# Later output turns, a moved PSUM bank and a shifted order of chunks in an attention and FFN kernel

## The reference

```python
x = x + xattn(layernorm(x), ctx, mask, padding)     # 32 query heads, 8 key groups, head size 16
#   q = X @ Wq.T + bq; k, v = ctx @ Wk.T + bk, ctx @ Wv.T + bv
#   w = softmax(where(mask, -inf, q k / 4)); out = (w v) @ Wo.T + bo
x = x + ternary_ffn(layernorm(x))                   # 512 -> 2048 -> 512
#   linear(x, w, g): rmsnorm(x) * g, rounded to 8 bits per token, times round(tanh(w / mean|w|))
#   h = silu(linear(x, w1)) * linear(x, w2); linear(h, w3)
x = x + attention_over_the_sequence(layernorm(x), ctx, ctx)
x = x + gated_ffn(layernorm(x))
```

## Time and profile before

| | us |
|---|---|
| median of 3 runs | 1564.48 (1561.67 to 1566.96) |
| profiled execution | 1560.04 |
| its span, first to last instruction | 1558.2 |
| busy PE, DVE, ACT, POOL | 1388.9, 806.3, 728.5, 481.5 |
| mean granted TensorE clock | 0.962 of full |

### The profile page before, as it was taken

How to read it: one execution, slowest core, us unless ns; L and a number is a source line. 1 busy time by engine, 2 the same in 40 slices (tenths; PEclk the granted TensorE clock), 3 DMA queues, 4 the chain that set the end, 5 groups by cost and what they waited for, 6 DMA issues and landing times. The chain is left out here.

```text
span 1558.2 us, 22502 instructions
## 1 busy us (share of the span) xinstructions
PE 1388.9 (89%) x8434; PEld 662.8 (43%) x8434; DVE 806.3 (52%) x1312; ACT 728.5 (47%) x1364; POOL 481.5 (31%) x522
## 2 busy tenths in 40 slices
PE   4788888788868999996899999989999999999998
PEld 4455555554533444552222222234444444444443
DVE  5864666566655878765666666624513211321220
ACT  3266666667664777771555555553501211210210
POOL 7211111446675775771322232144600000000000
PEclk9699999999988999997899999999999999999999
DMA  6646655656332010122644443223502002001000
GB/s 179 136 138 174 142 146 172 152 111 155 113 122 81 28 41 28 42 84 66 170 137 123 123 125 114 97 82 111 173 0 82 1 1 81 0 0 54 0 1 27
DMA packets 89446, 140.68 MB, mean 90 GB/s; under 512 B 8408, under 2 KB 47896, under 8 KB 88800
## 3 DMA queue, kind: packets, MB, share of 16 engines
q1 hardware_dynamic: 76544, 114.16, 26.8%
q10 hardware_dynamic: 12800, 25.17, 5.2%
HBM read 105.85 MB, written 33.46 MB: 89 GB/s over the span
## 5 line engine op out<-in xcount | busy, mean ns | idle before, releaser
L1785 DVE TENSOR_REDUCE c_negmax<-c_psA 128x1 f32<-128x512 f32 x256 | 165.7, 682 | 91.5 <-PE c_psA L1860 87.1
L2071 ACT ACTIVATE d_silu<-d_psGU 128x512 f32<-128x512 f32 x64 | 38.2, 596 | 344.3 <-PE d_psGU L2138 344.3
L2138 PE MATMUL d_psGU<-d_zt_hi,d_w_hi 128*128 128x512 bf16 x512 | 194.6, 380 | 3.8 <-ACT d_silu L2071 2.3
L2138 PE MATMUL d_psGU<-d_zt_hi,d_w_lo 128*128 128x512 bf16 x512 | 194.8, 380 | 0.0
L2138 PE MATMUL d_psGU<-d_zt_lo,d_w_hi 128*128 128x512 bf16 x512 | 194.8, 380 | 0.0
L1740 ACT ACTIVATE c_probs<-c_psB 128x512 f32<-128x512 f32 x256 | 140.4, 595 | 101.5 <-PE c_psB L1873 101.4
L2101 DVE TENSOR_TENSOR d_h<-d_psGU,d_silu 128x512 f32<-128x512 f32 x64 | 44.2, 691 | 221.2 <-PE d_psGU L2138 220.9
L894 DVE TENSOR_REDUCE a_negmax<-a_psX 128x4 f32<-128x1024 f32 x128 | 150.7, 1215 | 7.8 <-PE a_psX L1161 7.8
L753 ACT ACTIVATE a_probs<-a_psB 128x512 f32<-128x512 f32 x256 | 138.2, 593 | 24.8 <-PE a_psB L1173 24.5
L1860 PE MATMUL c_psA<-c_ks,c_qs 96*128 96x512 bf16 x256 | 103.8, 408 | 16.5 <-DVE c_negmax L1785 8.1
L672 POOL TENSOR_SCALAR ternary<-a_tern_stage 128x512 bf16<-128x512 f32 x48 | 91.6, 1924 | 77.4 <-ACT a_tern_stage L741 77.1
(11 more groups left out here) (231 smaller groups left out, 2559.0 us busy)
## 6 DMA issues: line engine op xcount, KB each, us to landing
a_tern_stage<-in_w ACTq DMA_DIRECT2D x32, 768.0 KB, 5.5
d_weight_stage<-in_w_last SPq DMA_DIRECT2D x24, 512.0 KB, 4.2
a_ks<-k_scr SPq DMA_DIRECT2D x8, 768.0 KB
a_qs<-q_scr SPq DMA_DIRECT2D x8, 768.0 KB
c_ks<-k_scr SPq DMA_DIRECT2D x48, 128.0 KB, 2.6
c_qs<-q_scr SPq DMA_DIRECT2D x48, 128.0 KB, 3.0
a_xz<-in_x SPq DMA_DIRECT2D x32, 128.0 KB, 3.1
a_ctx<-in_ctx_t SPq DMA_DIRECT2D x8, 512.0 KB, 4.7
```

The source lines that it names most:

```text
L1785: v.tensor_reduce(negm[:, u:u + 1], A[:, u % 2, :], AX.X, ALU.max, negate=True)\
L2138: last = pe.matmul(GU[:, 2 * up + i % 2, :], wgu[wh][:, i, up, k, :], zt[zh][:, k, :], start=(k == 0 and j == 0), stop=(k == DC - 1 and j ...
```

## The change

- Masked attention, order: in odd groups PE's `turn` goes from in front of the second scores to the end, in front of `weigh`, and DVE's `normalise` behind all reductions of the group. ACT's `out_high` goes from the start of an odd group to behind `results` of the even group before it (for the last chunk: from group 1 to group 0).
- Masked attention, inputs: DVE's statistics go from group 6 to 5, POOL's `scales` from 7 to 6 (in front of the additions of the output bias), ACT's `normalise` from the end of group 7 to the end of group 6.
- PSUM: keys and values are projected into bank 3 of X, not 2, and wait for the last maximum of the batch before and not for the copy of the transposed maxima. `transpose_max(b, 1)` goes behind the `turn` of group 0. The total of the weights' absolute values moves to a free corner of bank 2.
- Prologue: POOL's `inputs(1)` goes in front of `scales(1)`; DVE's `queries_low(1, 0)` and `(1, 1)` go between the first reductions.
- Ternary FFN: the down product of a chunk comes two parts after its transposition, not one; the x transposes go from part 1 to part 2. ACT takes the first x chunk after the first `scaled`, DVE the second after `largest(t, 0)`, and DVE's `update(t - 3)` goes from in front of `largest(t - 1, 1)` to behind `gate(t, 1)`.

```diff
@@ -441,7 +441,7 @@
...
         by_query = TURNED.rearrange("p (t r d) -> p t r d", t=ST, r=SHARE)
-        TOT = X[:, 3, 0:3]
+        TOT = X[:, 2, 300:303]
         MT = X[0:2 * HU, 2, :].bitcast(BF16)[:, 0:QJ * P]
@@ -636,8 +636,8 @@
...
                 g.memset(v1[i][:], 1.0).then_inc(s["ident"], 1)
+            inputs(1)
             scales(1)
-            inputs(1)
             g.memset(keep["ones"][:], 1.0).then_inc(s["ident"], 1)
@@ -656,7 +656,7 @@
...
                         inputs(b + 3)
-                    if grp == 7 and b + 3 < BATCH:
+                    if grp == 6 and b + 3 < BATCH:
                         scales(b + 3)
@@ -714,7 +714,7 @@
...
                 need(act, s["k_out"], n * 3 * DMA)
-                act.activation(k_hi[:], X[:, 2, 0:SEQ], ACT.Identity, bias=keep["bk"][:]).then_inc(s["k_hi"], 1)
+                act.activation(k_hi[:], X[:, 3, 0:SEQ], ACT.Identity, bias=keep["bk"][:]).then_inc(s["k_hi"], 1)
@@ -760,10 +760,6 @@
...
                     to, e = (b, 2 * g + 2) if g + 1 < GROUPS else (b + 1, 0)
-                    if g == 1 and b:
-                        out_high(b - 1, DC - 1)
-                    if g in (3, 5, 7):
-                        out_high(b, (g - 3) // 2)
                     if to < BATCH:
@@ -784,6 +780,10 @@
...
                     results(b, g)
+                    if g == 0 and b:
+                        out_high(b - 1, DC - 1)
+                    if g in (2, 4, 6):
+                        out_high(b, g // 2 - 1)
                     if b == TOTAL_AT and g == 1:
@@ -792,7 +792,7 @@
...
                         front.rounded(act, g - GROUPS + 2)
-                    if g == 7 and b + 3 < BATCH:
+                    if g == 6 and b + 3 < BATCH:
                         normalise(b + 3)
@@ -874,14 +874,14 @@
...
                 dve.wait_ge(s["k_hi"], n + 1)
-                v.scalar_tensor_tensor(out=k_lo[:], in0=X[:, 2, 0:SEQ], scalar=keep["bk"][:], in1=k_hi[:],
+                v.scalar_tensor_tensor(out=k_lo[:], in0=X[:, 3, 0:SEQ], scalar=keep["bk"][:], in1=k_hi[:],
                                        op0=ALU.add, op1=ALU.subtract).then_inc(s["k_lo"], 1)
...
                 v.tensor_tensor(v1[n % 3][:, :, :, 0:HD],
-                                X[:, 2, SEQ:2 * SEQ].rearrange("p (t g d) -> p t g d", t=ST, d=HD),
+                                X[:, 3, SEQ:2 * SEQ].rearrange("p (t g d) -> p t g d", t=ST, d=HD),
                                 keep["bv"][:].rearrange("p t (g d) -> p t g d", d=HD), ALU.add).then_inc(s["v_ready"], 1)
@@ -925,9 +925,9 @@
...
                         reduce_unit(b + 1, u)
-                    if g >= 1:
+                    if g % 2 == 0 and g:
                         normalise(b, g - 1)
-                    elif b:
+                    elif g == 0 and b:
                         normalise(b - 1, GROUPS - 1)
@@ -938,9 +938,11 @@
...
                         reduce_unit(b + 1, u)
+                    if g % 2:
+                        normalise(b, g - 1)
                     if more and g == 4:
                         split_max(b + 1, 0)
-                    if g == 6 and b + 3 < BATCH:
+                    if g == 5 and b + 3 < BATCH:
                         inputs(b + 3)
@@ -1026,10 +1028,10 @@
...
             second_ones()
-            queries_low(1, 0)
-            queries_low(1, 1)
             for u in range(HU):
                 reduce_unit(0, u)
+                if u < 2:
+                    queries_low(1, u)
             split_max(0, 0)
@@ -1089,15 +1091,15 @@
...
                 if n >= 2:
-                    pe.wait_ge(s["mt_copied"], 2 * (n - 1))
+                    pe.wait_ge(s["max_done"], MU * (n - 1))
                 for k in range(DC):
                     for i, (h, lo) in enumerate(halves):
-                        pe.matmul(X[:, 2, 0:SEQ], w[h, "wk"][:, k, :], (c_lo if lo else c_hi)[:, k, :],
+                        pe.matmul(X[:, 3, 0:SEQ], w[h, "wk"][:, k, :], (c_lo if lo else c_hi)[:, k, :],
                                   start=(k == 0 and i == 0), stop=(k == DC - 1 and i == 2))
...
                         for i, (h, lo) in enumerate(halves):
-                            last = pe.matmul(X[:, 2, SEQ + t * P:SEQ + (t + 1) * P],
+                            last = pe.matmul(X[:, 3, SEQ + t * P:SEQ + (t + 1) * P],
                                              (c_lo if lo else c_hi)[:, k, t * P:(t + 1) * P], w[h, "wv"][:, k, :],
@@ -1121,13 +1123,15 @@
...
-                    pe.wait_ge(s["v_ready"], min(b + 4, BATCH))
                     if b + 1 < BATCH:
...
                         pe.wait_ge(s["x_updated"], ST * b)
-                elif b + 1 == TOTAL_AT:
-                    pe.wait_ge(s["total"], 3)
+                    if b + 1 == TOTAL_AT:
+                        pe.wait_ge(s["total"], 3)
+                else:
+                    pe.wait_ge(s["v_ready"], min(b + 4, BATCH))
                 for k in range(DC):
@@ -1205,7 +1209,6 @@
...
                             turn_rows(n)
-                        transpose_max(b, 1)
                     if g == 1 and n is not None:
@@ -1214,16 +1217,19 @@
...
                         transpose_max(b + 1, 0)
-                    if g >= 1:
+                    if g % 2 == 0 and g:
                         turn(b, g - 1)
-                    elif b:
+                    elif g == 0 and b:
                         turn(b - 1, GROUPS - 1)
+                    if g == 0:
+                        transpose_max(b, 1)
                     if to < BATCH:
...
                         pe.wait_ge(s["total"], 1)
+                        pe.wait_ge(s["mt_copied"], 2 * (b + 1))
                         pe.matmul(TOT, keep["ones"][:], tot[:], start=True, stop=True).then_inc(s["total"], 1)
@@ -1231,6 +1237,9 @@
...
                         max_unit(b + 1, u)
+                    if g % 2:
+                        turn(b, g - 1)
                     weigh(b, g)
@@ -1434,9 +1443,9 @@
...
                     gate(t, 2)
-                take("x", t + 1, 0)
                 if 1 <= t <= NT:
                     scaled(t - 1, 0)
+                take("x", t + 1, 0)
                 if now:
@@ -1499,22 +1508,23 @@
...
                     gate(t, 0)
-                if t >= 3:
-                    update(t - 3)
                 if 1 <= t <= NT:
...
                     gate(t, 1)
+                if t >= 3:
+                    update(t - 3)
                 take("h", t - 2, 1)
...
                     gate(t, 2)
-                take("x", t + 1, 1)
                 next(ahead, None)
...
                     largest(t, 0)
+                take("x", t + 1, 1)
+                if now:
                     gate(t, 3)
@@ -1568,12 +1578,14 @@
...
                         product(t, n, 1, V, "h_done", "v_done")
-                    down(t - 3, NF - 1) if n == 0 else down(t - 2, n - 1)
-                    transposed("h", t - 2, n)
-                    if n == 1:
+                    down(t - 3, n + 2) if n < 2 else down(t - 2, n - 2)
+                    if n == 2:
                         for j in range(2):
                             transposed("x", t + 1, j)
-            down(NT - 1, NF - 1)
+                    transposed("h", t - 2, n)
+            for n in range(2, NF):
+                down(NT - 1, n)
 def build_sequence_attention(nc, io, keep, x_out, front, following):
```

## The result

The changed kernel takes 1556.13 us (median of 11 runs, 1551.73 to 1560.53), the kernel before 1565.38 in the same comparison (11 runs, 1561.15 to 1566.96). The ratio is 0.9944 (0.993 to 0.9958): about 9 us. The forecast had 18.5. Its sign was right and its range held the time, but the size was twice the true one.

A forecast was written before the change was run, and what follows sets the result against it. DVE's work was taken to pace attention groups 3 to 7 and a ring through POOL the FFN loop; savings of 2.0 + 8.4 + 1.8 + 0.5 + 5.9 = 18.6 us gave 1546 us, range 1531 to 1558.5.

The forecast's parts named there:

- Prologue: Before the attention: POOL's copies start at 29.65 in place of 31.76 us once its context split goes first; -2.0 us.
- Attention, group 3: Earlier `out_high`, then ACT binds: -0.1 us in each of batches 1, 2, 3, 5, 6; -1.0 in batch 0; -0.7 in batch 4.
- Groups 5 to 0: Attention: earlier inputs delay group 7, repaid by ready rows and keys in bank 3; -0.45 us for each of five batches.
- Batches 5 and 6: Attention without next inputs: transposed maxima behind the turn and group 1's late turn give 0.3 + 0.6 us each; -1.8.
- Late turning: Odd attention groups: late `turn` and `normalise` fall where PE waits for reductions anyway; 0, or 0.75 us a time without cover.
- FFN loop: Ternary FFN: PE's waits must go, but little becomes time; -0.3 us for each of six pairs of tiles, -1.8.
- ring through GpSimd: FFN loop: POOL's factors, ACT's rounding, DVE's gate and reductions, POOL again; closed by 28.8 us for two tiles.
- Tail: FFN drain of tiles 14 and 15: copy latency vanishes, the last tile's scale becomes the limit; -5.9 us.
- (a): Rival, FFN loop: PE's waits are the time; 9.8 us more gain, 1536 us; chance 0.13.
- (b): Rival, attention: all four waits are time; 41.7 us in place of 8.4, 1513 us; chance 0.05.
- (c): Rival, attention: it gives nothing, DVE and weight pieces bind; 1554 us, or 1557 with a smaller tail; chance 0.17.
- (d): Rival, odd attention groups: late `turn` idles DVE, 1.5 us in each of 21 groups; slower, 1586 us; chance 0.06.

The follow-up runs named there:

- e09: The kernel before with only GpSimd's `inputs(1)` put in front of `scales(1)`: 1560.88 us, 0.9975 of the kernel before.
- e13: The changed kernel with residual rows' loads cut to an eighth of their columns from batch 1 on: 1552.44 us, 0.9922 of the kernel before.
- e03: The changed kernel with ScalarE's one weight third in group 3 put behind the second exponentials and the results: 1547.15 us, 0.9876 of the kernel before.
- e04: The changed kernel with input statistics, scales and normalising back in groups 6, 7 and 7: 1548.51 us, 0.9897 of the kernel before.
- e10: The changed kernel with the edits of e03 and e04 together: 1537.95 us, 0.9833 of the kernel before.
- e08: The changed kernel loading an eighth of the columns of each FFN weight piece from the third on: 1547.03 us, 0.9896 of the kernel before.
- e05: The changed kernel with ScalarE's `out_high` back at the start of the odd groups: 1559.77 us, 0.9973 of the kernel before.
- e11: The changed kernel with the edits of e03, e04 and e06 together: 1536.75 us, 0.9824 of the kernel before.
- e06: The changed kernel with the odd groups' turning and normalising early again, in the even groups' place: 1549.26 us, 0.9909 of the kernel before.
- e14: The changed kernel with only VectorE's FFN `update` put back behind the first gate: 1579.98 us, 1.0092 of the kernel before.
- e12: The changed kernel with only ScalarE's normalising of batch b+3 back in group 7: 1551.76 us, 0.9915 of the kernel before.
- e02: The kernel before with only the edits of the ternary FFN, on all three engines: 1555.64 us, 0.9947 of the kernel before.
- e15: The changed kernel with only TensorE's order of the FFN products put back: 1603.77 us, 1.0250 of the kernel before.

## Why the prediction was half right

**Prologue (-2.0): right in size, by another course.** -2.6 in the profile, 3.9 with an interval of 2.0 to 5.8 in e09. GpSimd's copies start at 30.38 us, not at 29.65, as VectorE's mask copy came 0.7 later. VectorE's two copies of the constant rows and GpSimd's last one after are

```profile
33.05 6.49 DVE L998 COPY a_qs<-ones_row 32x8192 bf16<-32x8192 bf16 x1
39.46 9.10 DVE L999 COPY a_ks<-ones_row 32x8192 bf16<-32x8192 bf16 x1
```

```profile
37.33 9.08 POOL L646 COPY a_qs<-a_qs 64x8192 bf16<-64x8192 bf16 x1
```

where before VectorE's first began at 40.43 us and its second was

```profile
47.79 2.28 DVE L997 COPY a_ks<-ones_row 32x8192 bf16<-32x8192 bf16 x1
```

Before, only the first of VectorE's two collided with a copy of GpSimd, and now both do. GpSimd's last copy takes 2.1 us longer and ends 0.7 us later than before though it began earlier (46.41 for 45.72), while VectorE's last ends 1.5 us earlier (48.56 for 50.07), again 2.15 behind GpSimd's. The reductions follow on VectorE itself, so the gain is there, and not in GpSimd's copies, where the forecast had it. The Trainium skill (SBUF — State Buffer, the rule on the port pair) has the one that comes second stand still until the first is done; the 9.08 us of GpSimd's copy, which stood 7 us before, agree with it.

**Attention, group 3 (-0.5, -1.0, -0.7): the step that failed.** The forecast saw that "ACT then binds", and that its next third waits for a weight piece until 203.38, and gave 0.1 us a batch with the ends "nothing, and the full waits". Two things in it were wrong. It took the landing at 203.38 for fixed; it became 205.05, of which e13 puts 1.0 us to the residual loads that now go 2.8 us earlier. And it left out that all else on ScalarE stands in order behind that third and is needed earlier now. For batches 1 to 3, 5 and 6 together (groups 2 to 4) the term was -0.5; it is +3.8 in the pair of profiles, and between nothing and +4.6 when the three profiles of each attention are compared. With the third out of the way it is 7 to 9 us less than before (e03). Batch 0 gave 0.6 of its 1.0 in the pair, but took 48.2 to 52.5 us where the three profiles of before have 48.8 to 49.7; batch 4 lost 4.6 where 0.7 was to be won, in part by its groups 5 to 7 and by the clock. That the term could turn round could have been read from the profile: ScalarE's wait of 1.71 us in the earlier trace rows was hidden only as long as what it held up was needed later than it ended, and the edit made it needed 1.5 us earlier.

**Groups 5 to 0 (-0.45 for each batch): near as a sum, wrong in worth.** Counting from `weigh` of group 0, the forecast had `weigh` of group 6 at 37.9 us, of group 7 at 43.4 and of the next batch at 49.6. Less the 2.6 us lost in group 4, the changed kernel has 37.5, 43.8 and 49.9. In those terms a batch has 0.3 us more than forecast. But e04 shows that the edit was worth a loss: without it a batch takes 48.1 to 48.9 us (e10), with it 50.3 to 50.7 (e03). The forecast compared with the kernel before alone, and never with the change less this part; a part whose sum comes out near nothing is a part to look at by itself.

**Batches 5 and 6 (-1.8): half of it.** -0.8 in the pair, and -0.9 with groups 2 to 4 left out. The -4.1 of e03 and e08 lies almost all in groups 2 to 4, which this term was not about. **Batch 7 (-2.2): right**, 37.76 to 35.40 (35.4 to 36.1 for 37.3 to 37.8 in the six profiles). **Behind it**, from the last `weigh` to the last output product, 2.3 us went that no term had (11.3 to 9.0; 2.3 to 3.4 in the six profiles). Before, TensorE paused for 2.97 us and was at half clock from 464 to 470 us (granted 0.50), so that the first nine matmuls of the output product start some 0.43 us apart; e05, with the same pause, has the same. In the changed kernel that pause is 1.02 us, the clock is full (1.00 from 467 to 473) and they start 0.216 apart. The first two of before and of after:

```profile
467.07 0.61 PE L1133 MATMUL a_psX<-attn_w_hi,a_out_hi 128*128 128x512 bf16 x1 [0.94 <-DVE a_out_lo L858]
467.47 0.63 PE L1133 MATMUL a_psX<-attn_w_hi,a_out_lo 128*128 128x512 bf16 x1
```

```profile
470.01 0.39 PE L1137 MATMUL a_psX<-attn_w_hi,a_out_hi 128*128 128x512 bf16 x1 [0.93 <-DVE a_out_lo L858]
470.23 0.38 PE L1137 MATMUL a_psX<-attn_w_hi,a_out_lo 128*128 128x512 bf16 x1
```

**Late turning (0):** nothing that can be told in e11 beside e10, 5.5 us in the changed kernel beside e06. The forecast named its cover (TensorE waits for reductions anyway) and the price without it, 0.75 us a time; the cover held, but the pause it lengthened could cost clock, which it had not counted. Batch 4 (59.68 for 55.03) is where that shows most.

**FFN loop (-0.3 for two tiles): right in size, wrong about the waits.** 28.83 to 28.42 us over four pairs of tiles, -0.4. The forecast held that TensorE's "waits must go". Those for the evictions went, but the update, now later, put others in their place, on TensorE's down product of the same two tiles as the earlier trace rows:

```profile
554.88 1.02 PE L1570 MATMUL b_psD<-ternary,b_hq_t 128*128 128x512 bf16 x4 [1.92 <-DVE a_ctx_halves L1502]
...
568.22 1.02 PE L1570 MATMUL b_psD<-ternary,b_hq_t 128*128 128x512 bf16 x4 [0.21 <-DVE a_ctx_halves L1502]
```

That is 2.1 us for two tiles, where it was 1.9, and in the 144 us from 523 to 667 TensorE is idle for 11.4 us in place of 9.6. So the change didn't test what these waits are worth. What speaks for the forecast's ring through GpSimd is e14, which disturbs it and lengthens the tiles.

**First tiles (-0.5): right.** From the last output product to the first up product of tile 4 it is 57.6 us for 58.2 (57.5 to 57.8 in eight profiles with the new FFN, 59.6 to 59.7 in e05, e08 and e12). What is missing lies further on, from tile 12 to tile 15: 43.5 us for 41.9, so in eight profiles with the new FFN, but 41.8 in e02, e03 and e04. TensorE pauses there for the update in e02 as in the changed kernel, and only in the latter do the four matmuls behind the pause take longer; the windows from 669 to 673 us show the clock (changed kernel, then e02):

```profile
668.65 1.45 PE L1570 MATMUL b_psD<-ternary,b_hq_t 128*128 128x512 bf16 x4 [2.03 <-DVE a_ks L1502]
669.00:673.00 4.00, 4.00 (x19) 3.15 (x17) 1.45 (x3) 2.96 (x6) 3.82 (x6) 0.57 0.17 66
```

```profile
669.07 1.02 PE L1561 MATMUL b_psD<-ternary,b_hq_t 128*128 128x512 bf16 x4 [1.98 <-DVE a_ks L1493]
669.00:673.00 4.00, 3.93 (x25) 2.58 (x26) 1.49 (x3) 3.38 (x7) 3.73 (x7) 1.00 0.17 66
```

**Tail (-5.9): right**, 6.1, step 1.30 us. Its working put 1.35 us of that to the update's place; e15 leaves 0.7 for it and e14 gives it 4.3, so it is no fixed share. The mark "no PE wait above 0.2" was not met: 0.62, 0.81 and 0.50 us are left.

**Rivals.** (a), the loop's waits as time, came out neither way: two tiles take 28.4 us and 27.2 would have been needed, but TensorE's idle time never went. (b), all four waits as time, fell: TensorE's wait for `out_low` did go (31.2 to 1.3), and the attention got longer. The Trainium skill (Perfetto Trace Analysis, on optimising what leaves the matmul engine idle) says to optimise the engines that block the critical path; here removing what the wait named was not that, as 5.0 us of waits for the exponentials became 35.1. (c), "the attention gives nothing, as DVE and the weight pieces bind throughout", came nearest. It had 0.17, and its 1554 is 2 us from the median. It was ranked below the forecast though both rested on the same row. Its "throughout" doesn't hold, as e10's attention takes 376.6 us, and its nothing was a loss of 1.8 to 4.3. (d) did not happen: VectorE's wait at the reciprocal, 21.3 us before, is 9.2 after; the late turning costs in another way. Of the marks named ahead, `weigh` of group 7 later in its batch and L1064's wait below 8 us were met, and "a batch above 51" told the attention's forecast wrong with 54.62 and 52.52, though the kernel before has 51.76 and 51.21 itself. That TensorE's waits of the loop would be gone was not met.

## What to carry to other kernels

When an edit lets one engine run ahead, follow everything that it releases: the transfers that start earlier and what they will run beside, and the queue of the engine that must then wait. A wait for a transfer that is hidden today is a bound of the change, with a sign, not a cover. When a wait is removed, look whether the engine's idle time went with it or only changed its name, as it did here in the attention and in the FFN loop. And cost each part of a bundle against the bundle without it: here two parts of it cost 17 us, and the change without them gives 26 us in place of 9. A single profile of each kernel could not have told that batch 1's step of 9.29 us is not the change's; kernels that share the stage could.

## What the runs showed of the hardware

A piece of 768 KB of weights took 5.1 to 5.3 us from its issue to its use in batch 2 when four loads of 128 KB were issued 5.3 to 5.5 us behind it (four profiles), 6.4 to 6.9 with them issued 2.5 to 2.7 us behind it (three), and 5.9 with these cut to an eighth. In batches 3 and 4 of these three, with the loads about as close, it took 5.3 to 6.0, as in the four (5.4 to 6.1). The same pause of TensorE did not always have the same consequence: after 1.84 us the clock fell in the changed kernel (the 16 matmuls took 1.69 us), and in e12, after 1.84 us at the same place of the same batch, it did not (1.07 us); in the FFN it was 0.57 after a pause of 2.03 us in the changed kernel and 1.00 after 1.98 in e02. What made the difference these rows don't show, so such a cost can be bounded ahead of a run, here by 0.6 us for a `weigh` and 1.7 us for half an output product, but not be told.
